# Where TensorE's queue issues the query-major scores in each attention step of an audio tower block

## The chip, the cores and the metric

The program runs on one core of a Trainium2 chip. The metric is the device time of one execution in microseconds (us), taken as the median of several runs; lower is better.

## The reference, cut to what matters

The input of 32 x 1024 samples is cut into patches of 16, which gives 2048 tokens (64 for each of 32 batch rows). Three stages follow, all in float32:

```python
h = silu(x_cat @ W_h.T + b_h) @ W_o.T + b_o + x_cat @ W_r.T + b_r      # (2048, 256)
# attention, 16 heads of 16, over the 64 tokens of one batch row
q, k, v = (einsum('bshd,ed->bshe', layernorm(h), W) for W in (Wq, Wk, Wv))
h = h + softmax(q k^T / sqrt(256)) v @ W_out.T + b_out
# a frequency-domain product; for real input it is one 256 x 256 matrix and a bias
h = h + real(ifft(fft(layernorm(h)) @ w_freq)) + bias
```

## The kernel before, in words

The 2048 tokens are 16 tiles of 128 tokens (two batch rows each); T is 16. A first stage (to about 44 us) makes h for all tiles. From then on one step per tile does the attention and the frequency product, software-pipelined: in `step(i)` each engine works at several tiles at once.

TensorE's queue is written out by hand: `step(i)` at line 1213 calls the parts in a fixed order, and each part first waits on semaphores for its inputs. An engine works its queue strictly in that order. The parts, with their lines:

- `turn_side(i-1)`, line 1096 (matmuls at 1101): two transposes of the residual tile h2, wanted by the frequency product.
- `turn_max(i+1)`, line 1089 (matmul at 1093): one transpose of the row maxima.
- `turn_x(i+3)`, line 1174 (matmuls at 1180): two transposes of the normalized tile. In step 1, tile 4 is turned ahead of the side. These are the three turns.
- `scores(i+2)`, line 1052 (matmuls at 1058), behind the two waits of `scores_inputs(i+2)`, line 1048: the query-major scores of tile i+2, 16 small matmuls of 32 rows by 64 columns of the array, which a profile shows as 32 records. They go to columns 0 to 255 of banks 0 to 3 and serve for nothing but the row maxima.
- `keyed_scores(i+1)` (1073) and `take_max(i+1)` (1085): the key-major scores of tile i+1 in columns 256 to 511 of the same banks, and the maxima taken off.
- `mix_freq(i-1)` (1133 with the leading part, 1137 with the rest), `project(i)` (1166 leading, 1170 rest), `query(i+3)` (1189 to 1191).
- `weigh(i+1)`, line 1105 (sums at 1113, weighing at 1120), the last of the step.

ScalarE (ACT), `step` at 404: `copy_max(i+1)` (374), `copy_side(i-1)` (388, 391), `copy_xT(i+3)` (358), `lead_on(i)` (395), `exponent(i+1)` (380, four), `copy_q(i+3)` (368), `copy_xzT(i+3)` (363, two). VectorE (DVE), `step` at 896: `divide(i)` (853 to 867), `variance2(i-1)` (890, 894), `split_x(i+3)` (789), four `maximum(i+2)` (835), `split_max(i+2)` (842, 844), `residual(i)` (886, makes h2), `finish(i-1)` (877, makes y). A `maximum` of tile i+2 waits for its scores and, besides, for the exponent of tile i+1 on the same bank (line 834). GpSimd (POOL), `step` at 604: `place_same(i+2)` (552), `split_side(i-1)` (591), `split_on(i)` (602), `inv_std2(i-1)` (566, 570), `add_bias(i-1)` (576), `normalize(i+4)` (584). SyncE (SP) issues two transfers of `place_crossed(i+2)` (297) and one store (289) in each step.

Of the kernel before, what the change touches and what calls it, by code (L numbers as in the profile page):

```python
# [24 lines left out]
T = BATCH * TOK // P  # L25
# [3 lines left out]
QUADS = 4  # L29
# [34 lines left out]
def audio_tower_kernel(nc, a, out):  # L64
    with ExitStack() as ctx:
# [3 lines left out]
        def sem(name):  # L69
            return ctx.enter_context(nc.semaphore(name))  # L70
# [145 lines left out]
        scores_done, max_done, max_turned, max_copied = (  # L216
            sem("scores_done"), sem("max_done"), sem("max_turned"), sem("max_copied"))
# [718 lines left out]
        def _(pe):  # L936
# [111 lines left out]
            def scores_inputs(t):  # L1048
                pe.wait_ge(xzT_copied, 2 * (t + 1))
                pe.wait_ge(q_copied, t + 1)  # L1050

            def scores(t):

                for half in range(HALF):
                    for b in range(2):
                        for j in range(QUADS):
                            rows32 = slice(32 * j, 32 * j + 32)
                            last = pe.matmul(bank[j][TOK * b:TOK * b + TOK, half * P:(half + 1) * P],  # L1058
                                             qT[t % 3][rows32, half, TOK * b:TOK * b + TOK],
                                             xzT[t % 3][rows32, 2 * half + b, :, :].rearrange("p e k -> p (e k)"),  # L1060
                                             start=True, stop=True)
                            if half == HALF - 1 and b == 1:
                                last.then_inc(scores_done, 1)

            def keyed_scores(t):

                for half in range(HALF):
                    for b in range(2):
                        for j in range(QUADS):
                            rows32 = slice(32 * j, 32 * j + 32)  # L1070
                            at0 = D + half * P + TOK * b
                            for e in range(2):
                                pe.matmul(bank[j][TOK * e:TOK * e + TOK, at0:at0 + TOK],  # L1073
                                          xzT[t % 3][rows32, 2 * half + b, e, :],
                                          qT[t % 3][rows32, half, TOK * b:TOK * b + TOK],
                                          start=(half == 0 and b == 0), stop=False, skip_group_check=True)

            def take_max(t):

                pe.wait_ge(max_copied, HALF * (t + 1))  # L1080
                if t == 0:
                    pe.wait_ge(minus_set, 1)
                for j in range(QUADS):
                    rows32 = slice(32 * j, 32 * j + 32)
                    pe.matmul(bank[j][:, D:2 * D], minus_rows[rows32, :],  # L1085
                              maxT[rows32, :, :].rearrange("p h q -> p (h q)"),
                              start=False, stop=True, skip_group_check=True).then_inc(keyed_done, 1)

            def turn_max(t):
                pe.wait_ge(max_lo_set, t + 1)  # L1090
                if t == 0:
                    pe.wait_ge(h_copied, T - 1)
                pe.transpose(bank[MAX_BANK][:, 0:P], max_terms[:].rearrange("p j r -> p (j r)").bitcast(F32),  # L1093
                             ident[:]).then_inc(max_turned, 1)

            def turn_side(t):
                pe.wait_ge(h2_done, t + 1)
                if t == T - 1:
                    pe.wait_ge(side_copied, t)
                for half in range(HALF):  # L1100
                    last = pe.transpose(bank[SIDE_BANK][:, D + half * P:D + (half + 1) * P],  # L1101
                                        h2[t % 2][:, half * P:(half + 1) * P], ident[:])
                last.then_inc(side_turned, 1)
# [21 lines left out]
            def mix_freq(t):  # L1125
                pe.wait_ge(side_copied, t + 1)
                if t == 0:
                    pe.wait_ge(mix_split, 1)
                if t >= 1:
                    pe.wait_ge(y_set, t)  # L1130
                for half in range(HALF):
                    for w in (mix_hi, mix_lo):
                        pe.matmul(bank[FREQ_BANK][:, D:2 * D], side_hi[:, half * P:(half + 1) * P], w[:, half, :],  # L1133
                                  start=(half == 0 and w is mix_hi), stop=False)
                pe.wait_ge(side_lo_set, t + 1)
                for half in range(HALF):
                    last = pe.matmul(bank[FREQ_BANK][:, D:2 * D], side_lo[:, half * P:(half + 1) * P], mix_hi[:, half, :],  # L1137
                                     start=False, stop=(half == HALF - 1))
                last.then_inc(freq_done, 1)
# [12 lines left out]
            def project(t):  # L1152
                if t == 0:
                    pe.wait_ge(mix_kept, 1)
                if t >= WHOLE_ON:
                    pe.wait_ge(on_set, t + 1)
                    for half in range(HALF):
                        last = pe.matmul(bank[LAST_PROJ_BANK if t == T - 1 else PROJ_BANK][:, 0:D], onT[:, half, :],  # L1158
                                         value_whole[:, half, :],
                                         start=(half == 0), stop=(half == HALF - 1))  # L1160
                    last.then_inc(proj_done, 1)
                    return
                pe.wait_ge(on_hi_set, t + 1)
                for half in range(HALF):
                    for w in (value_hi, value_lo):
                        pe.matmul(bank[PROJ_BANK][:, 0:D], on_hi[:, half, :], w[:, half, :],  # L1166
                                  start=(half == 0 and w is value_hi), stop=False)
                pe.wait_ge(on_lo_set, t + 1)
                for half in range(HALF):
                    last = pe.matmul(bank[PROJ_BANK][:, 0:D], on_lo[:, half, :], value_hi[:, half, :],  # L1170
                                     start=False, stop=(half == HALF - 1))
                last.then_inc(proj_done, 1)

            def turn_x(t):
                pe.wait_ge(xh_set, t + 1)
                if t >= 1:
                    pe.wait_ge(q_copied, t)
                    pe.wait_ge(xzT_copied, 2 * t)
                for half in range(HALF):
                    last = pe.transpose(bank[X_BANK][:, half * P:(half + 1) * P], xh[t % 2][:, half * P:(half + 1) * P],  # L1180
                                        ident[:])
                last.then_inc(x1_turned, 1)

            def query(t):
                pe.wait_ge(x_lo_set, t + 1)
                if t == 0:
                    pe.wait_ge(score_split, 1)
                out_q = bank[QUERY_BANK][:, D:2 * D]
                pe.matmul(out_q, score_hi[:], x_hi[:], start=True, stop=False)
                pe.matmul(out_q, score_lo[:], x_hi[:], start=False, stop=False)  # L1190
                pe.matmul(out_q, score_hi[:], x_lo[:], start=False, stop=True).then_inc(q_done, 1)  # L1191
# [19 lines left out]
                pe.matmul(half, halfway[:, 1, c * P:(c + 1) * P], sine[:], start=False, stop=True).then_inc(mixw_done, 1)  # L1211

            def step(i):
                if i == 1:
                    turn_x(4)
                if i >= 1:
                    turn_side(i - 1)
                if 0 <= i + 1 < T:
                    turn_max(i + 1)
                if 0 <= i < T - 3 and i != 1:  # L1220
                    turn_x(i + 3)
                if 0 <= i + 2 < T:
                    scores_inputs(i + 2)
                    scores(i + 2)
                if 0 <= i + 1 < T:
                    keyed_scores(i + 1)
                    take_max(i + 1)
                if 1 <= i < T - 2:
                    mix_freq(i - 1)
                if i >= 0:  # L1230
                    project(i)
                if 0 <= i + 3 < T:
                    query(i + 3)
                if i == -1:
                    cols_spectrum(1)
                if 0 <= i + 1 < T:
                    weigh(i + 1)
# [40 lines left out]
            for i in range(-1, T - 1):  # L1278
                step(i)
# [37 lines left out]
```

## Time and profile before

| | |
|---|---|
| median of 3 runs | 139.19 us (138.58 to 139.27) |
| the profiled execution, its own time | 140.0 us |
| its span in the trace | 138.2 us |
| TensorE busy | 130.9 us, 95% |
| VectorE / ScalarE / GpSimd busy | 111.2 / 91.4 / 94.2 us |
| granted TensorE clock | 1.0 throughout |

Times are us from the start of the span. A row of the timeline gives start, duration, engine, line and operation, what is written from what is read, the shape and the count; brackets at its end tell how long the engine had been idle before it and who ended that. PE is TensorE's matmuls, PEld its weight loads. The duration of one matmul includes its way through the array, so consecutive matmuls overlap, and what a matmul costs is read from start to start. The end of a matmul is modelled.

### The profile page before, as it was taken

How to read it: one execution, taken by the hardware profiler on the slowest of the kernel's cores; microseconds unless marked ns; L12 is line 12 of the kernel's file. 1: busy time of each engine (PE TensorE's matmuls, PEld its weight loads, DVE VectorE, ACT ScalarE, POOL GpSimd, SP SyncE). 2: the span in 40 equal slices, each digit the busy share in tenths (PEclk: the TensorE clock that was granted, in tenths of full speed). 3: DMA queues.
4: the chain of work that ended last, by engine and by line, in shares of the span. 5: the costliest groups of instructions: out<-in, count | busy, mean ns of one | idle time of the engine just before them, and what ended most of it. 6: DMA issues, size and time to landing. Idle time of an engine off the chain costs nothing.

```text
span 138.2 us, 7034 instructions
## 1 busy us (share of the span) xinstructions
PE 130.9 (95%) x2891; PEld 110.1 (80%) x2891; DVE 111.2 (80%) x337; ACT 91.4 (66%) x261; POOL 94.2 (68%) x186
## 2 busy tenths in 40 slices
PE   6899999999999999999999999999999999998980
PEld 2389999999997876988888888788888888886640
DVE  4685499869979579897898898988988988988850
ACT  5376475478878676886867867768778678666110
POOL 3285895999547364678678787786796787774660
PEclk9999999999999999999999999999999999999999
DMA  3667000030000020221312302203112123031012
GB/s 62 164 159 261 20 0 0 5 34 9 2 0 5 5 24 0 24 48 21 62 38 24 61 15 50 55 12 66 44 18 57 47 24 61 1 66 43 0 47 72
DMA packets 24512, 5.89 MB, mean 43 GB/s; under 512 B 20384, under 2 KB 24224, under 8 KB 24480
## 3 DMA queue, kind: packets, MB, share of 16 engines
q1 hardware_dynamic: 24192, 5.31, 17.9%
q8 instruction: 23, 0.38, 1.2%
q10 hardware_dynamic: 288, 0.13, 0.4%
q14 instruction: 9, 0.07, 0.2%
HBM read 2.29 MB, written 2.10 MB: 32 GB/s over the span
## 4 chain that ended last, share of the span: by engine, by line
PE 77%; POOL 8%; issue 4%; DVE 4%; ACT 3%; ACTq 1%; POOLq 0%; DVEq 0%
PE bank L978 10%; PE bank L1073 7%; PE bank L1058 6%; PE bank L1113 5%; PE bank L983 5%; PE bank L1133 5%; PE bank L1120 4%; PE bank L1166 4%; PE bank L1101 3%; PE bank L972 3%; PE bank L1085 3%; PE bank L1170 2%; PE bank L1180 2%; PE bank L1137 2%; PE bank L1158 2%
## 5 line engine op out<-in xcount | busy, mean ns | idle before, releaser
L835 DVE TENSOR_REDUCE bank<-bank 128x4 f32<-128x256 f32 x64 | 22.8, 425 | 7.2 <-ACT pT L380 7.0
L380 ACT ACTIVATE pT<-bank 128x256 f32<-128x256 f32 x64 | 19.4, 390 | 3.8 <-PE bank L1085 3.6
L591 POOL TENSOR_TENSOR side_lo<-sideT,side_hi 128x256 fp32r<-128x256 f32 x14 | 10.3, 732 | 13.4 <-ACT sideT L391 13.4
L1073 PE MATMUL bank<-qT,xzT 32*64 32x64 f32 x1024 | 16.3, 234 | 0.0
L552 POOL TENSOR_SCALAR xblk<-xh,parity_sb 128x128 f32<-128x128 f32 x32 | 11.5, 375 | 6.9 <-PE bank L1120 5.6
L705 DVE TENSOR_TENSOR hid_lo<-bank,hid_hi 128x512 fp32r<-128x512 f32 x16 | 10.9, 684 | 6.3 <-ACT bank L342 6.3
L1073 PEld LDWEIGHTS bank<-qT,xzT 32*64 32x64 f32 x1024 | 15.5, 130 | 0.3 <-issue 0.2
L374 ACT ACTIVATE maxT<-bank,parity_sb 128x128 fp32r<-128x128 f32 x32 | 10.0, 363 | 8.6 <-PE bank L1093 8.6
L560 POOL TENSOR_TENSOR hb_all<-h_all,bout_bc 128x256 f32<-128x256 f32 x16 | 11.6, 740 | 3.9 <-ACT h_all L346 3.9
L341 ACT ACTIVATE hid_hi<-bank 128x512 fp32r<-128x512 f32 x16 | 9.6, 599 | 5.3 <-PE bank L972 5.3
L368 ACT ACTIVATE qT<-bank 128x256 f32<-128x256 f32 x16 | 6.2, 386 | 9.6 <-PE bank L1191 9.6
L978 PE MATMUL bank<-wo_hi,hid_hi 128*128 128x256 f32 x64 | 11.7, 303 | 0.2
L576 POOL TENSOR_TENSOR h2b<-h,fbias_bc 128x256 f32<-128x256 f32 x16 | 11.7, 734 | 0.3 <-DVE h L886 0.3
L1120 PEld LDWEIGHTS bank<-pT,xblk 128*32 128x32 f32 x512 | 9.5, 110 | 2.7
L363 ACT ACTIVATE xzT<-bank,parity_sb 128x256 f32<-128x256 f32 x28 | 11.7, 472 | 0.0
L1058 PE MATMUL bank<-xzT,qT 32*64 32x128 f32 x512 | 11.1, 280 | 0.2 <-DVE hid_lo L705 0.2
L570 POOL TENSOR_TENSOR rstd<-ve,half_neg 128x1 f32<-128x1 f32 x16 | 9.1, 570 | 2.2
L602 POOL TENSOR_TENSOR on_lo<-onT,on_hi 128x256 fp32r<-128x256 f32 x14 | 10.4, 741 | 0.1
L1113 PE MATMUL bank<-pT,pair_ones_sb 128*32 128x256 f32 x128 | 10.2, 391 | 0.0
L983 PE MATMUL bank<-wo_hi,hid_lo 128*128 128x256 f32 x64 | 10.2, 281 | 0.0
L978 PE MATMUL bank<-wo_lo,hid_hi 128*128 128x256 f32 x64 | 10.1, 282 | 0.0
L1120 PE MATMUL bank<-pT,xblk 128*32 128x64 f32 x512 | 10.1, 219 | 0.0
(170 smaller groups left out, 379.4 us busy)
## 6 DMA issues: line engine op xcount, KB each, us to landing
out<-y SPq DMA_DIRECT2D x16, 128.0 KB, 1.7
xblk<-xh SPq DMA_DIRECT2D x32, 32.0 KB, 2.5
wo_raw<-in_W_o SPq DMA_DIRECT2D x1, 512.0 KB, 4.1
wout_raw<-in_W_out SPq DMA_DIRECT2D x1, 256.0 KB, 3.0
fr<-in_wr SPq DMA_DIRECT2D x1, 256.0 KB, 4.2
fi<-in_wi SPq DMA_DIRECT2D x1, 256.0 KB, 4.4
bout_bc<-in_b_out SPq DMA_DIRECT2D x1, 128.0 KB, 3.4
cosine_sb<-in_cosine SPq DMA_DIRECT2D x1, 128.0 KB, 4.2
```

The lines of the kernel that those rows point to most:

```text
L363: nc.scalar.activation(xzT[t % 3][:, :, e, :], bank[X_BANK][:, 0:D].rearrange("p (g k) -> p g k", k=TOK), ACT.Copy, scale=parity[:, e:e + ...
L380: nc.scalar.activation(pT[:, j, :], bank[j][:, D:2 * D], ACT.Exp).then_inc(exp_done, 1)
L552: last = nc.gpsimd.tensor_scalar(xblk[t % 2][:, b, :].rearrange("p (g e d) -> p g e d", e=2, d=HD)[:, :, b, :], xh[t % 2][:].rearrange("p ...
L560: nc.gpsimd.tensor_tensor(hb_all[:, t, :], h_all[:, t, :], bout_bc[:], ALU.add).then_inc(hb_done, 1)
L576: nc.gpsimd.tensor_tensor(h2b[t % 2][:], h2[t % 2][:], fbias_bc[:], ALU.add).then_inc(h2b_done, 1)
L835: nc.vector.tensor_reduce(rowmax[:, j, :], bank[j][:, 0:D].rearrange("p (h k) -> p h k", k=TOK), AX_X, ALU.max).then_inc(max_done, 1)
L978: pe.matmul(bank[MIX_BANK[par]][:, 0:D], hid_hi[:, par, c * P:(c + 1) * P], w[:, c, :], start=(t < 2 and c == 0 and w is wo_hi), stop=False)
L983: last = pe.matmul(bank[MIX_BANK[par]][:, 0:D], hid_lo[:, par, c * P:(c + 1) * P], wo_hi[:, c, :], start=False, stop=(t > 0 and c == NC - 1))
L1058: last = pe.matmul(bank[j][TOK * b:TOK * b + TOK, half * P:(half + 1) * P], qT[t % 3][rows32, half, TOK * b:TOK * b + TOK], xzT[t % 3][row ...
L1073: pe.matmul(bank[j][TOK * e:TOK * e + TOK, at0:at0 + TOK], xzT[t % 3][rows32, 2 * half + b, e, :], qT[t % 3][rows32, half, TOK * b:TOK * b ...
L1113: last = pe.matmul(sums[32 * j:32 * j + 32, D:2 * D], pair_ones[:], pT[:, j, :], start=True, stop=True)
L1120: last = pe.matmul(bank[PV_BANK][32 * j:32 * j + 32, cols], xblk[t % 2][:, b, half * P + 32 * j:half * P + 32 * j + 32], pT[:, j, cols], s ...
```

## The change

In steps 0 to 13 the scores of tile i+2 with their input waits are issued first, directly behind `weigh(i)` of the step before and ahead of the turns, and a wait for all maxima of tile i+1 (`max_done`) is put ahead of them. Before, `turn_max(i+1)`, which waits for the split maxima, stood ahead and implied it. Step -1 keeps its order. Nothing else is changed; no instruction is added but the wait.

```diff
             def step(i):
+                if 0 <= i and i + 2 < T:
+                    pe.wait_ge(max_done, QUADS * (i + 2))
+                    scores_inputs(i + 2)
+                    scores(i + 2)
                 if i == 1:
                     turn_x(4)
                 if i >= 1:
@@ -1219,7 +1223,7 @@
                     turn_max(i + 1)
                 if 0 <= i < T - 3 and i != 1:
                     turn_x(i + 3)
-                if 0 <= i + 2 < T:
+                if i == -1:
                     scores_inputs(i + 2)
                     scores(i + 2)
                 if 0 <= i + 1 < T:
```

## Rows read from the trace of the kernel before

**Rows 1.** The page: busy time and share of each engine.

```profile
PE 130.9 (95%) x2891; PEld 110.1 (80%) x2891; DVE 111.2 (80%) x337; ACT 91.4 (66%) x261; POOL 94.2 (68%) x186
```

**Rows 2.** The chain that ended last, over step 9 (start us, us, what).

```profile
97.83 0.45 PE bank L1120 x32
98.28 0.37 PE bank L1101 x2
...
98.97 0.62 PE bank L1058 x32
...
103.25 0.45 PE bank L1120 x32
```

**Rows 3.** Windows: steps 5 to 13 with their boundary, and the end.

```profile
core 0: us, PE busy (x) PEld busy (x) DVE busy (x) ACT busy (x) POOL busy (x), PEclk, DMA share, GB/s
...
70.86:119.89 49.03, 49.03 (x1447) 41.93 (x1441) 43.76 (x136) 36.66 (x118) 37.30 (x72) 1.00 0.21 40
...
124.95:138.20 13.25, 8.67 (x137) 5.77 (x137) 7.43 (x20) 3.13 (x10) 5.19 (x10) 1.00 0.13 41
```

**Rows 4.** Timeline where step 8 ends and step 9 begins.

```profile
97.30 0.38 ACT L368 ACTIVATE qT<-bank 128x256 f32<-128x256 f32 x1 [0.77 <-PE bank L1191]
...
97.58 0.83 ACT L363 ACTIVATE xzT<-bank,parity_sb 128x256 f32<-128x256 f32 x2
...
98.20 0.20 PEld L1101 LDWEIGHTS bank<-ident,h 128*128 128x128 f32 x2
```

**Rows 5.** Timeline of step 13's start.

```profile
119.61 0.48 ACT L363 ACTIVATE xzT<-bank,parity_sb 128x256 f32<-128x256 f32 x1
119.89 0.20 PEld L1101 LDWEIGHTS bank<-ident,h 128*128 128x128 f32 x2
```

**Rows 6.** Timeline of step 1's start, where a turn waits for an ACT copy.

```profile
53.76 0.48 ACT L363 ACTIVATE xzT<-bank,parity_sb 128x256 f32<-128x256 f32 x1
...
54.35 0.20 PEld L1180 LDWEIGHTS bank<-ident,xh 128*128 128x128 f32 x2 [0.41 <-issue]
```

**Rows 7.** Timeline of step 3's start, which waits for the residual.

```profile
64.95 0.48 ACT L363 ACTIVATE xzT<-bank,parity_sb 128x256 f32<-128x256 f32 x1
...
65.43 0.20 PEld L1101 LDWEIGHTS bank<-ident,h 128*128 128x128 f32 x2 [0.30 <-DVE h L886]
```

**Rows 8.** Timeline of step 9: turn, scores, key-major scores.

```profile
98.70 0.27 PE L1180 MATMUL bank<-ident,xh 128*128 128x128 f32 x1
...
98.90 0.69 PE L1058 MATMUL bank<-xzT,qT 32*64 32x128 f32 x32
...
99.39 1.01 PE L1073 MATMUL bank<-qT,xzT 32*64 32x64 f32 x64
```

**Rows 9.** Timeline of the first stage's end: scores followed by a full-array matmul.

```profile
41.69 0.70 PE L1058 MATMUL bank<-xzT,qT 32*64 32x128 f32 x32 [0.16 <-DVE hid_lo L705]
...
42.32 0.10 PEld L989 LDWEIGHTS bank<-wr_termsT,x_termsT 128*128 128x128 bf16 x1 [0.17 <-issue]
```

**Rows 10.** Timeline of step 8: the side's remainder and its reader.

```profile
94.63 0.73 POOL L591 TENSOR_TENSOR side_lo<-sideT,side_hi 128x256 fp32r<-128x256 f32 x1 [0.84 <-ACT sideT L391]
...
95.68 0.31 PEld L1137 LDWEIGHTS bank<-mix_hi,side_lo 128*128 128x128 f32 x2
```

**Rows 11.** Timeline of step 0: TensorE waits for a POOL remainder.

```profile
51.45 0.74 POOL L602 TENSOR_TENSOR on_lo<-onT,on_hi 128x256 fp32r<-128x256 f32 x1
...
52.24 0.30 PEld L1170 LDWEIGHTS bank<-value_hi,on_lo 128*128 128x128 f32 x2 [0.22 <-POOL on_lo L602]
```

**Rows 12.** The chain that ended last, steps 13 and 14.

```profile
124.15 0.74 POOL h2b L576
...
124.92 0.48 DVE y L877
...
127.04 1.13 PE bank L1158 x4
```

**Rows 13.** Waits: line waited for, total us, times, longest us.

```profile
DVE bank L835 <- ACT pT L380: 7.0, 15, 1.6
...
PEld bank L1101 <- DVE h L886: 1.0, 3, 0.4
```

## The prediction

> **What bounds the kernel now.** I first read the page: TensorE is busy for 95% of the span [rows 1]. Busy time alone proves little for overlapping matmuls, so I read the chain that ended last next. Over a steady step it never leaves TensorE: each group starts where the one before it ended, and from one weighing to the next it takes 103.25 - 97.83 = 5.42 us [rows 2]. The windows say the same: from the start of step 4 at 70.86 to that of step 13 at 119.89 are 9 steps in 49.03 us, and no moment without a matmul [rows 3]. So in steps 4 to 13 whatever is added between two matmuls is added to the time, and nothing is there to be won by filling waits. Only steps 0 to 3 and the end have short waits.
>
> **What moves.** In steps 0 to 13 the 16 scores matmuls (32 records) go ahead of turn_side, turn_max and turn_x in TensorE's queue. They issue no DMA, and no instruction on ACT, DVE, POOL or SP changes its place. The scores' own price, 0.49 us from start to start [rows 8], is paid before and after. Their consumers gain nothing from having them early: `maximum` also waits for the exponent of the tile before, and it is this that ends its wait 15 times [rows 13]; that exponent hangs on take_max, still behind the turns. The new wait on max_done costs nothing: the maxima are done before the residual starts, which in its turn is done before the turns start. Three things do cost.
>
> **Term 1, the inputs of the scores.** The scores of step i read xzT and q of tile i+2, which ACT copies at the end of step i-1: query ends, copy_q starts at 97.30, the two xzT copies run from 97.58 for 0.83 us, to 98.41 [rows 4]. TensorE meanwhile has only the weighing, and is ready for the next step at 98.20. Before, three turns covered the copy. From the end of such a copy to TensorE's first weight load that waited for it are 54.35 - (53.76 + 0.48) = 0.11 us [rows 6]. So the scores start at 98.52, a wait of 0.32. I took it for the steps 2 to 13, 12 of them; the last reads 119.61 + 0.48 + 0.11 - 119.89 = 0.31 [rows 5]. In step 3 the kernel already stands for the residual, to 65.43, and the copy would be usable at 64.95 + 0.48 + 0.11 = 65.54: only 0.11 is new there [rows 7]. Step 1 already waits for this same copy ahead of turn_x(4) [rows 6], and step 0 has its copies long before. The sum is 11 x 0.32 + 0.11 = 3.6 us. The stall doesn't repay itself: the next query is behind the scores, and the next copies behind that query. Queued behind the waiting scores are all three turns, and behind those ACT's copies of maxima, side and x.
>
> **Term 2, one more change of the array's shape.** Turns use the full array (128*128), scores and keyed scores tiles of 32*64, so scores to keyed is free now. A turn costs 0.11 and the scores start 0.20 behind the last turn's start, so full to small costs 0.09 [rows 8]; after the change turn to keyed scores pays that in its place. New is scores to turn. The trace has that direction once, where the first scores precede a full-array matmul: 42.32 - 41.69 = 0.63, against 0.49 in front of keyed scores [rows 8, 9], so 0.14. It could be as little as 0 if that row hid some other wait, or as much as 0.20 if everything must leave the array (98.90 + 0.69 - 99.39, the modelled end against the next start [rows 8]). I take 0.14, the one direct row. Times 14 steps, 2.0 us. The step from weighing to scores replaces weighing to turn and lies under the wait of term 1, in which the array empties anyway. The Trainium skill, "TensorEngine Tiling (Array Packing)", section "Tiling Modes", says that changing the tiling mode drains the TensorE. With a whole drain for each added change the term would be 14 x 0.20 = 2.8 us; the row speaks for less, since the weight load at 42.32 comes before the modelled end at 42.39 [rows 9].
>
> **Term 3, the side's remainder loses its cover.** turn_side starts a relay: ACT copies maxima, then side twice, POOL makes side_lo, and TensorE's second part of mix_freq reads it. Now POOL is done at 94.63 + 0.73 = 95.36 and TensorE loads it at 95.68 [rows 10]: 0.32 of slack, less the 0.05 that TensorE needed after a POOL remainder in step 0 (52.24 - 51.45 - 0.74 [rows 11]). With the scores no longer between turn_side and mix_freq TensorE arrives 0.49 earlier in the relay's time: 0.49 - 0.32 + 0.05 = 0.22 us of wait, in steps 1 to 13. The bounds are 0 (if the relay also shrinks) and 0.33 (if the wake-up takes 0.11 more before the matmul itself can start, then late by that much). on_lo, behind side_lo on POOL, is late by no more than that, so the wait at mix_freq covers it. The maxima keep cover: two copies of ACT against turn_x and about 0.9 us of keyed scores.
>
> **The end.** Behind step 13 the chain leaves TensorE: it runs over POOL's h2b, DVE's y and divide, to project(14) at 127.04 [rows 12]. This relay counts from turn_side(13), which now comes 0.32 + 0.49 + 0.14 = 0.95 later after the weighing. So step 13 counts 0.95 instead of 0.68. Nothing in steps 14 and 15 gives the 0.49 back.
>
> **The sum.** Step 0: 0.14. Step 1: 0.14 + 0.22 = 0.36. Steps 2 to 12: 11 x (0.32 + 0.14 + 0.22) = 7.48, less 0.21 in step 3. Step 13: 0.95. Together 8.7 us. The profiled execution took 140.0 (span 138.2, 1.8 around it) and would take 148.7. The median of the runs is 0.8 below that execution, so I forecast 139.2 + 8.7 = 147.9 us. A steady step would be 6.1 us instead of 5.42.
>
> **The rivals.**
> 1. *The relay of the side keeps up*, terms 1 and 2 only. For it: 0.22 is a difference of small numbers, and the order of ACT might shift in TensorE's favour. 14 x 0.14 + 3.6 + 0.49 = 6.1, so 145.3. Chance 0.15.
> 2. *Only the shape change costs*, if ACT's copies are in time after all. Against: they end after the weighing in every step from 2 on [rows 4, 5]. 139.2 + 2.0 = 141.2. Chance 0.05.
> 3. *POOL and DVE close a longer loop.* h2b, y, divide and onT all hang on turn_side, and if they also come late for the next on_hi, each step pays more than 6.1. For it: that relay bounds the end now [rows 12]. Against: ACT reaches on_hi only behind five copies that themselves wait for the turns, so onT may come later together with them. At an assumed 0.15 more in each of 12 steps, 149.7. Chance 0.07.
> 4. *The clock falls.* With two waits per step TensorE might be granted 1.2 instead of 2.4 GHz, and a half-clock step would cost up to 5 us more: beyond 153. Against: over the last 13.25 us it is busy for only 8.67 and is granted 1.00 throughout [rows 3]. Chance 0.02.
> 5. *Faster.* turn_side waits for DVE's residual three times, 1.0 us in all by the weight loads [rows 13]; the scores would cover that. It decides if the xzT copies end before the weighing and the added shape change is free. Then about 0.5 of it is true gain (the rest is pipelining of the loads): 138.7. Against: rows 4 has the copy 0.21 too late before any wake-up. Chance 0.03.
> 6. *Gain and cost cancel*, a small cost of shapes against that same gain, 139.2. Chance 0.01.
>
> **How the numbers follow.** The forecast has 0.67. About 0.5% either way is what a measurement of this kernel can tell from no change, 0.7 us. Faster has rival 5, 0.03; same takes rival 6 and the part of rival 2 in which the shape change costs next to nothing, 0.02; slower is the rest, 0.95. The range takes in rival 1 with a shape change at half price (145.3 - 1.0 = 144.3) and, above, the whole drain (+0.8) and the longer wake-up of term 3 (13 x 0.11 = 1.4): 150.1. Outside stand most of rival 2 and rivals 4 to 6, some 0.1, and the cases in which I mis-sized the terms by more than their bounds, which I put at another 0.1.
>
> **What would show it.** Each step right: weight loads of L1058 wait for ACT xzT about 0.3 in 12 steps; 0.63 from scores to the first turn; L1137 waits for POOL side_lo about 0.2; a steady period of 6.1; clock 1.00. Wrong: a period under 5.6 with L1058 directly behind the weighing, which would mean that the copies aren't late; or L1137 without a wait, which is rival 1; or waits at L1166 or L1170 for onT's copies, which is rival 3.

## The result, and the profile after

| | before | after |
|---|---|---|
| median | 139.23 us (4 runs, 138.58 to 140.02) | 147.63 us (4 runs, 147.06 to 148.18) |
| ratio | | 1.058, 95% interval 1.054 to 1.063 |
| profiled execution, own time / span | 140.0 / 138.2 us | 147.31 / 144.8 us |
| first to last weighing group (L1120), 15 steps | 80.00 us | 88.11 us |

The forecast was 147.9 us with a range of 144.3 to 150.1. On the median the change costs 8.4 us, and 8.1 by the ratio. The spans differ by only 6.6 us, because two things outside the steps differ between these two executions: the first stage ended 0.43 us earlier in the one of after, and from the end of the last y to the end of the span it took 2.2 us against 3.3. The steps themselves are the 8.11 us to explain. The ratios here leave out an execution that took over 1.5% longer than the fastest of its kernel; there is one, 142.19 us, and it is the profiled one of `shape_in_changed`.

First the page of after, its busy line; it answers to [rows 1].

```profile
PE 134.7 (93%) x2891; PEld 109.1 (75%) x2891; DVE 112.6 (78%) x337; ACT 89.8 (62%) x261; POOL 94.3 (65%) x186
```

The same instructions, and TensorE is now busy for 93% where it was busy for 95%: that says nearly nothing. The chain that ended last does, over one steady step; it answers to [rows 2].

```profile
101.96 0.45 PE bank L1120 x32
102.41 0.23 issue
102.64 0.70 PE bank L1058 x32
103.34 0.37 PE bank L1101 x2
103.71 0.11 PE bank L1093
103.82 0.22 PE bank L1180 x2
104.03 0.84 PE bank L1073 x53
104.88 0.32 PE bank L1085 x4
105.20 0.67 PE bank L1133 x4
105.87 0.03 issue
105.90 0.50 PE bank L1137 x2
```

Two "issue" entries are new, 0.23 behind the weighing and 0.03 in front of L1137. "Issue" is time for which the profile shows nobody to wait for. What ended each has to be read from the timeline of after around them: ACT's copy, and POOL's remainder.

```profile
101.71 0.83 ACT L363 ACTIVATE xzT<-bank,parity_sb 128x256 f32<-128x256 f32 x2
101.78 0.63 PE L1120 MATMUL bank<-pT,xblk 128*32 128x64 f32 x32
...
102.61 0.48 PEld L1058 LDWEIGHTS bank<-xzT,qT 32*64 32x64 f32 x32 [0.37 <-issue]
...
103.27 0.44 PE L1101 MATMUL bank<-ident,h 128*128 128x128 f32 x2
...
103.97 0.91 PE L1073 MATMUL bank<-qT,xzT 32*64 32x64 f32 x64
...
104.81 0.39 PE L1085 MATMUL bank<-maxT,minus_rows_sb 32*128 32x256 f32 x4
...
105.11 0.74 POOL L591 TENSOR_TENSOR side_lo<-sideT,side_hi 128x256 fp32r<-128x256 f32 x1 [1.53 <-ACT sideT L391]
```

The copies end at 101.71 + 0.83 = 102.54, and the first load of the scores comes at 102.61. From the weighing group to the scores are 0.86 us (101.78 to 102.64). In the kernel before it is 0.56 from the weighing to the turns, in the timeline of [rows 4]:

```profile
97.65 0.63 PE L1120 MATMUL bank<-pT,xblk 128*32 128x64 f32 x32
...
98.21 0.44 PE L1101 MATMUL bank<-ident,h 128*128 128x128 f32 x2
```

POOL's remainder ends at 105.11 + 0.74 = 105.85, and L1137 starts at 105.90. The other new wait is named in the list of waits of after (total us, times, longest us).

```profile
PEld bank L1058 <- issue: 5.0, 14, 0.4
...
PEld bank L1137 <- POOL side_lo L591: 3.2, 13, 0.3
```

It comes 13 times, mostly with 0.24, once in each of the steps 1 to 13, which are those with a turn of the side and this second part of `mix_freq`. The windows of after give 9 steady steps, from the scores of step 4 to those of step 13.

```profile
core 0: us, PE busy (x) PEld busy (x) DVE busy (x) ACT busy (x) POOL busy (x), PEclk, DMA share, GB/s
...
72.29:126.89 54.60, 52.17 (x1440) 41.58 (x1440) 45.35 (x136) 35.70 (x117) 37.38 (x72) 1.00 0.19 36
```

54.60 / 9 = 6.07 us a step at a granted clock of 1.00, against 49.03 / 9 = 5.45 in [rows 3]. (The 5.45 contains one pause of TensorE; without it the step is 5.42.)

### The profile page after: what moved, and what is told of

Read it like the earlier page. It is cut to its first block, busy times and chain, and to the rows that moved or that the text cites. A ratio compares the mean times of both kernels' runs of the same rounds, so it can differ in the third digit from the quotient of the medians.

```text
span 144.8 us, 7034 instructions
## 1 busy us (share of the span) xinstructions
PE 134.7 (93%) x2891; PEld 109.1 (75%) x2891; DVE 112.6 (78%) x337; ACT 89.8 (62%) x261; POOL 94.3 (65%) x186
## 4 chain that ended last, share of the span: by engine, by line
PE 78%; issue 6%; POOL 4%; DVE 3%; ACT 3%; DMA 3%; ACTq 1%; SPq 0%; POOLq 0%; DVEq 0%
PE bank L978 10%; PE bank L1073 7%; PE bank L1058 6%; PE bank L1113 6%; PE bank L1133 5%; PE bank L983 5%; PE bank L1137 4%; PE bank L1120 4%; PE bank L1166 4%; PE bank L1101 3%; PE bank L972 3%; PE bank L1085 3%; DMA xblk<-xh 3%; PE bank L1180 2%; PE bank L1170 2%
## 5 line engine op out<-in xcount | busy, mean ns | idle before, releaser
L1073 PE MATMUL bank<-qT,xzT 32*64 32x64 f32 x1024 | 14.7, 231 | 0.0
L1073 PEld LDWEIGHTS bank<-qT,xzT 32*64 32x64 f32 x1024 | 12.6, 130 | 2.5 <-issue 2.5
L1058 PEld LDWEIGHTS bank<-xzT,qT 32*64 32x64 f32 x512 | 7.7, 131 | 5.5 <-issue 5.0
L1120 PEld LDWEIGHTS bank<-pT,xblk 128*32 128x32 f32 x512 | 9.5, 110 | 2.8
L789 DVE TENSOR_TENSOR x_lo<-bank,x_hi 128x256 fp32r<-128x256 f32 x16 | 6.8, 424 | 6.1 <-ACT x_hi L358 5.9
L584 POOL TENSOR_SCALAR xh<-h_all,rstd,shift 128x256 f32<-128x256 f32 x16 | 8.9, 554 | 2.4 <-DMA xblk<-xh 1.7
```

Of the source, the lines that this page charges most:

```text
L1073: pe.matmul(bank[j][TOK * e:TOK * e + TOK, at0:at0 + TOK], xzT[t % 3][rows32, 2 * half + b, e, :], qT[t % 3][rows32, half, TOK * b:TOK * b ...
L1120: last = pe.matmul(bank[PV_BANK][32 * j:32 * j + 32, cols], xblk[t % 2][:, b, half * P + 32 * j:half * P + 32 * j + 32], pT[:, j, cols], s ...
```

## The experiments

Steps are measured from one L1120 group to the next (in kernels with two more lines ahead of it, L1122). A steady step is one of steps 4 to 12 without a pause of TensorE; the pauses are in the last section. "Sum" is the 15 steps from the first such group to the last, in the profiled execution. Ratios are to the kernel before on the same chip.

### The waits alone: waits_only

```diff
             def step(i):
+                if 0 <= i and i + 2 < T:
+                    pe.wait_ge(max_done, QUADS * (i + 2))
+                    scores_inputs(i + 2)
                 if i == 1:
                     turn_x(4)
```

> The order of the kernel before, with only the waits (maxima, xzT and q of tile i+2) put at the head of steps 0 to 13; the scores stay behind the turns. Theory of three additive terms: only term 1 is left, 11 x 0.30 + 0.1 in step 3 and 0.3 at the end, so about 139.2 + 3.6 = 142.8 us, a steady period of 5.73, and no wait at L1137. Rival, a closed loop over ACT and POOL sets the period of 6.06 as soon as TensorE is late for the turns: near 147, with a wait at L1137. Rival, the late start is won back because the turns and scores are short: under 140.

Measured: 141.81 us, ratio 1.016 (1.012 to 1.020); sum 83.14, steady step mostly 5.68 to 5.70. In this kernel the profile names the releaser, at the matmul of the turn behind the waits; its timeline at a step's start:

```profile
99.58 0.63 PE L1120 MATMUL bank<-pT,xblk 128*32 128x64 f32 x32
100.44 0.41 PE L1101 MATMUL bank<-ident,h 128*128 128x128 f32 x2 [0.23 <-ACT xzT L363]
```

The wait for xzT is real by itself and adds 0.27 to the step: 0.30 in front of the turn, less 0.03 that the turns then take less. L1137 doesn't wait: from L1133 to it are 0.58 us, as in the kernel before. So there is no closed loop that would take the step to 6.06. The ratio gives 2.2 us (1.6 to 2.8), the trace 3.1; what may lie between them is in the last section.

### The input wait taken away: no_input_wait

```diff
                     pe.wait_ge(max_done, QUADS * (i + 2))
-                    scores_inputs(i + 2)
-                    scores(i + 2)
+                    scores_inputs(i + 1)
+                    scores(i + 1)
```

> The changed order, but the scores at the head of step i read tile i+1 (its copies are a whole step old), so the maxima belong to the wrong tile; the same matmuls are issued. Three additive terms: term 1 goes, L1120 to L1058 is 0.56 instead of 0.86, so 12 x 0.30 = 3.6 less than the changed kernel, about 144.0 us, period 5.76, L1137 still waits 0.24. Rival, a closed loop over ACT and POOL: the wait reappears further down the step and the time stays near 147.5.

Measured: 143.51 us, ratio 1.028 (1.023 to 1.032); sum 84.39, steady step 5.75. The scores stand directly behind the weighing now, 0.56 behind the start of its group:

```profile
99.80 0.63 PE L1120 MATMUL bank<-pT,xblk 128*32 128x64 f32 x32
100.36 0.69 PE L1058 MATMUL bank<-xzT,qT 32*64 32x128 f32 x32
```

Term 1 is 0.31 a step, and it goes without coming back elsewhere. The wait for `max_done` is still in this kernel, so it costs nothing. Step 7 alone has 6.14, by a pause in its keyed scores.

### The remainder waits taken away: no_remainder_waits and no_side_wait

```diff
-                pe.wait_ge(side_lo_set, t + 1)
                 for half in range(HALF):
-                    last = pe.matmul(bank[FREQ_BANK][:, D:2 * D], side_lo[:, half * P:(half + 1) * P], mix_hi[:, half, :],
+                    last = pe.matmul(bank[FREQ_BANK][:, D:2 * D], side_hi[:, half * P:(half + 1) * P], mix_hi[:, half, :],
...
-                pe.wait_ge(on_lo_set, t + 1)
                 for half in range(HALF):
-                    last = pe.matmul(bank[PROJ_BANK][:, 0:D], on_lo[:, half, :], value_hi[:, half, :],
+                    last = pe.matmul(bank[PROJ_BANK][:, 0:D], on_hi[:, half, :], value_hi[:, half, :],
```

`no_remainder_waits` has both hunks, and a wait on ACT for the side_lo of the tile before, ahead of the side_hi copy, which is long fulfilled. `no_side_wait` has the first hunk alone.

> The changed order, but mix_freq and project read side_hi and on_hi again in place of the remainders side_lo and on_lo, without waiting for them (POOL still computes them); the products lose their low-order part. Three additive terms: term 3 goes, which the trace of the changed kernel shows as 0.19 + 0.12 = 0.31 a step, 13 times: 4.0 less, about 143.6 us, period 5.75; the scores' wait for xzT stays at about 0.3. Rival, closed loop: the wait grows at another place and the time stays above 146.5.

Measured: 143.77 us, ratio 1.030 (1.026 to 1.035); sum 84.16, steady step 5.75. Term 3 is 0.31 a step too. The sum has two things besides. Step 0 is 0.29 shorter (4.64 against 4.93), because its wait for on_lo, which the kernel before has too [rows 11], is left out as well. And at the end nothing is won: step 13 is 0.35 shorter and step 14 is 0.35 longer.

> The changed order; only mix_freq reads side_hi again in place of side_lo, without its wait; project still waits for on_lo, which POOL makes right behind side_lo. I expect nearly nothing: on_lo lands 0.70 behind side_lo, and TensorE reaches L1170 0.70 behind L1137, so the wait moves from L1137 to L1170: 147.4 us, with about 0.3 at L1170. Rival, only the wait for side_lo counts, as my term 3 had it: 4.0 less, 143.6 us.

Measured: 148.25 us, ratio 1.061 (1.056 to 1.067); sum 87.97, steady step 6.06, as in the changed kernel. Its list of waits has in place of L1137's the following row (L1169 is this kernel's second part of `project`):

```profile
PEld bank L1169 <- POOL on_lo L602: 3.2, 14, 0.3
```

The wait is the same size one group later. POOL finishes on_lo 0.70 us behind side_lo and TensorE reaches the one group 0.70 behind the other, so the two waits are one lateness, and the profile shows only the one met first. Who had read L1137 off the list and mended that alone would have gained nothing.

### Only the order left: shape_in_changed

The edits of `no_input_wait` and `no_remainder_waits` together.

> The changed order without the input wait (scores read tile i+1) and without both remainder waits (side_hi and on_hi read again), so only the order itself is left. If the terms are additive: 147.6 - 3.6 - 4.0 = 140.0 us, period about 5.46, of which the shape change is 14 x 0.04 and the rest the end's relay. If the shape change costs 0.14 net: 141.2. If something else in the order costs: more than 141.5.

Measured: 139.88 us, ratio 1.000 (0.997 to 1.003), 10 runs; sum 80.62, steady step 5.44 to 5.45. In the trace the new order alone costs 0.03 in a steady step. The other steps are not alike. Step 0 is 0.27 shorter than before, since the on_lo wait of the kernel before is left out here too. Step 3 is 0.18 shorter (5.45 against 5.63), since the scores now cover the wait for the residual. Steps 13 and 14 are 0.21 and 0.41 longer. Without the pauses of both traces (some 0.4 us here, 0.25 before) it adds up to 0.4 us, at the edge of what the runs resolve; with the gain of step 0, which isn't the order's, set aside it would be 0.7. The steps of this profiled execution begin later, the first L1120 at 49.98 against 48.1 to 48.8 in the other profiles, so that its span is no measure of them. The timeline of one step's start shows the parts:

```profile
98.97 0.63 PE L1122 MATMUL bank<-pT,xblk 128*32 128x64 f32 x32
99.53 0.69 PE L1060 MATMUL bank<-xzT,qT 32*64 32x128 f32 x32
100.15 0.44 PE L1103 MATMUL bank<-ident,h 128*128 128x128 f32 x2
```

### Two changes of shape more: shape_only

```diff
                     turn_max(i + 1)
-                if 0 <= i < T - 3 and i != 1:
-                    turn_x(i + 3)
                 if 0 <= i + 2 < T:
                     scores_inputs(i + 2)
                     scores(i + 2)
+                if 0 <= i < T - 3 and i != 1:
+                    turn_x(i + 3)
```

> The order of the kernel before, with the scores moved ahead of turn_x alone: turn_side, turn_max, scores, turn_x, keyed scores. Their inputs are ready there (0.39 behind the weighing's end against 0.32), and the scores still stand between turn_side and mix_freq, so only the added change of the array's shape is left, in 12 steps. By the 0.14 of my term 2: 139.2 + 1.7 = 140.9 us. By what the trace of the changed kernel shows (scores 0.14 longer, keyed scores 0.10 shorter, net 0.04): 139.7 us, period 5.46. By a whole drain of 0.20: 141.6.

Measured: 140.90 us, ratio 1.009 (1.006 to 1.012), 8 runs; sum 81.97, steady step 5.59 to 5.60. The timeline of a steady step of this kernel:

```profile
99.69 0.27 PE L1093 MATMUL bank<-ident,max_terms 128*128 128x128 f32 x1
99.89 0.69 PE L1058 MATMUL bank<-xzT,qT 32*64 32x128 f32 x32
100.52 0.44 PE L1180 MATMUL bank<-ident,xh 128*128 128x128 f32 x2
100.88 0.84 PE L1073 MATMUL bank<-qT,xzT 32*64 32x64 f32 x58
```

The expectation was badly set up. By parting the three turns this kernel has two changes of shape more than the kernel before: turns, scores, turn, keyed scores. The changed kernel has only one more. Read as two it fits: 0.63 - 0.49 = 0.14 from scores to turn; 0.36 for two transposes and the way into the keyed scores, where two transposes alone take 0.22, so 0.14; and keyed scores that take 0.84 and not 0.94, 0.10 less. That is 0.18 a step, and 5.60 - 5.42 is 0.18. By the ratio it is 1.2 us (0.8 to 1.6) over 12 steps, by the trace 2.0. That the median, 140.9, is the very number expected from 0.14 a step is a coincidence: two changes stand behind it, not one.

### Repairs that leave nothing out: query_early, side_first, both_repairs

```diff
+                if 0 <= i and i + 3 < T:
+                    query(i + 3)
                 if i >= 0:
                     project(i)
-                if 0 <= i + 3 < T:
+                if i == -1:
                     query(i + 3)
```

> The changed order, and query(i+3) ahead of project(i) in steps 0 to 12, so that ACT copies q and xzT 0.7 us earlier; nothing is left out. Three additive terms: xzT is there before the weighing ends, term 1 goes by a change that computes everything: 3.6 less, about 144.0 us, and L1137 still waits. Rival, ACT is still in the exponents: then copy_q starts at their end, and part of the wait stays, 145.5. Rival, closed loop: 147.

Measured: 143.64 us, ratio 1.029 (1.023 to 1.035); sum 83.96, steady step 5.76. The copies now end at 98.61 + 0.83 = 99.44 in the step where the weighing group starts at 99.38, well before the scores at 99.94:

```profile
98.61 0.83 ACT L363 ACTIVATE xzT<-bank,parity_sb 128x256 f32<-128x256 f32 x2
...
99.38 0.63 PE L1120 MATMUL bank<-pT,xblk 128*32 128x64 f32 x32
...
99.94 0.23 PEld L1058 LDWEIGHTS bank<-xzT,qT 32*64 32x64 f32 x16
```

Term 1 is gone by another way than in `no_input_wait` and is worth the same in a steady step. Step 0 gains 0.26 besides (4.67 against 4.93), since `query` there stands in front of the group that waits for on_lo and covers the wait.

```diff
                 if i + 1 < T:
-                    copy_max(i + 1)
+                    act.wait_ge(max_turned, i + 2)
                 if i >= 1:
                     copy_side(i - 1)
+                if i + 1 < T:
+                    copy_max(i + 1)
```

> The changed order; on ACT the two side copies go ahead of the two maxima copies, once the turn of the maxima is done (nothing is left out). The side reaches POOL two copies (0.5 us) earlier, so the wait at L1137 (0.31 a step with its loads) goes; the maxima come 0.5 later, for which the trace of the changed kernel has about 0.4 of cover in front of L1085, so up to 0.2 may come back there. By additive terms: period 5.75 to 5.95, 2 to 4 us less than the changed kernel, 143.5 to 145.5 us. Rival, a closed loop over ACT and POOL: 147.5.

Measured: 147.74 us, ratio 1.059 (1.052 to 1.065); sum 88.13, steady step 6.02 to 6.05: a miss. The wait for the side is gone, and one for the maxima has come, in its list of waits (L1087 is this kernel's `take_max`):

```profile
PEld bank L1087 <- ACT maxT L374: 5.4, 14, 0.6
...
PE bank L1087 <- ACT maxT L374: 3.5, 14, 0.4
```

The keyed scores take 1.11 us to take_max instead of 0.84. I had given the maxima 0.4 of cover; it was 104.81 - (103.85 + 0.63) = 0.33, less the wake-up, and they were moved back by two copies, 0.5. As I read it, ACT's copies behind the turns take about as long as the work that TensorE has left in front of their readers, so whichever reader is served last waits: 0.31 a step for the side, 0.27 for the maxima.

> The changed order with query ahead of project and the side copies ahead of the maxima copies; nothing is left out. Additive terms: 147.6 - 4.0 (term 1, as measured) - 2 to 4 (as side_first), so 139.8 to 141.6 us, period 5.46 to 5.65. It can't beat the kernel before, whose period is TensorE's own 5.42. Rival: with both repairs some wait that was hidden comes out, and the time is above 142.5.

Measured: 144.01 us, ratio 1.032 (1.025 to 1.039); steady step 5.73, hardly less than the 5.76 of `query_early` alone. The expectation counted a gain that `side_first` doesn't have.

### The end: last_step_old

```diff
-                if 0 <= i and i + 2 < T:
+                if 0 <= i and i + 3 < T:
                     pe.wait_ge(max_done, QUADS * (i + 2))
...
-                if i == -1:
+                if i in (-1, T - 3):
                     scores_inputs(i + 2)
```

> The changed order in steps 0 to 12, the old order in step 13. In the changed kernel step 13 took 0.88 more than before and step 14 0.07 more; both should go: 147.6 - 0.9 = 146.7 us. Rival, the end's relay over POOL and DVE absorbs what step 13 adds: no change, 147.6.

Measured: 146.20 us, ratio 1.047 (1.041 to 1.053); sum 87.18, with 4.84 for step 13 and 4.40 for step 14, which before are 4.83 and 4.39. The new order in step 13 costs 0.93 in the trace; the medians differ by 1.4 us and the ratios by 1.1%, 1.5 us, with intervals of half a per cent each way.

### Both kernels once more: before_again, after_again

> The kernel before, profiled once more, to see how much of its trace repeats: from the first to the last L1120 group 80.0 us again, a period of 5.42, and whether the 3.3 us between the last y and the end of the span (2.2 in the changed kernel's trace) belong to the kernel or to this one execution.

Measured: 140.76 us, span 139.0; the sum is 81.10, not 80.00. The period is 5.40 to 5.43 in all the steps 4 to 12 but two. From the end of the last y to the end of the span it takes 2.2 us, as in all other profiles, so the 3.3 of the first profile belonged to that one execution and not to the kernel.

> The changed kernel, profiled once more, for the same purpose: 88.1 us from the first to the last L1120 group, a period of 6.06, and 2.2 us from the last y to the end.

Measured: 147.91 us, span 145.2, sum 88.10 again, and 2.2 us from the last y to the end. What makes before's sum differ is in the last section.

## Why the prediction was right

The sum of the steady step closes from separate runs. Before 5.42; the order alone +0.03 (`shape_in_changed`); the inputs of the scores +0.31 (6.06 - 5.75, `no_input_wait`; `query_early` says 0.30); the remainders +0.31 (6.06 - 5.75, `no_remainder_waits`): 6.07, measured 6.06. So in the steady steps the terms add up; each wait lies at another place of TensorE's queue. At the end they don't: there `no_remainder_waits` only moved 0.35 from step 13 to step 14. Point by point:

- **What bounds the kernel** held: with the waits of terms 1 and 3 taken out of the changed order the steady step is 5.45 against 5.42 and the ratio 1.000. The ratio flatters a little, since the wait of step 0, 0.27, is left out with them.
- **Nothing is won by early scores** held. In the changed order the maxima wait for the exponent all the same, and a steady step has no part that became shorter but the keyed scores.
- **Term 1** was right: 0.32 forecast, 0.31 by the run. Of its parts the wake-up, from the copy's end to TensorE's load, was 0.07 and not 0.11, and the matmul then stands 0.03 behind its load. That three turns covered the copies before isn't right: `turn_x(i+3)` waits for the same copies of tile i+2 itself, and in step 9 of the kernel before its first load stands at 98.52, 0.11 behind their end at 98.41. Two turns covered them and little was to spare, which doesn't change the term. In step 3 the wait of before for the residual was covered as forecast: 5.63 became 6.06, 0.43 more, where the other steady steps have 0.64.
- **Term 2** was mis-sized: 0.14 a step forecast, 0.03 measured. The 0.14 from scores to turn is there to the digit (103.27 - 102.64 = 0.63). The step that failed is the sentence that scores to keyed scores "is free now". It wasn't: the keyed scores take 0.94 behind the scores and 0.84 behind a turn, so that 0.10 of the new price comes back. Why they take less behind a turn no run shows. The Trainium skill, "TensorEngine Tiling (Array Packing)", section "Tiling Modes", has a drain at each change of mode. The traces agree that a change between the turns and the small tiles costs something in either direction, 0.09 to 0.14, and `shape_only`, which has two more of them, pays 0.14 for each. In the changed order 0.10 of the added price is given back, which no count of mode changes shows.
- **Term 3** was mis-sized the other way: 0.22 forecast, 0.31 measured. The place and the cause were right. The wait is 0.19 in front of L1137 (0.77 from L1133 where before are 0.58). The rest, 0.11, comes behind it: load and matmul of L1137 start together at 105.90, so the matmul hasn't its load done in advance, and L1137 to L1166 is 0.34, not 0.23. That is the upper bound that the prediction named and didn't take. The timeline of [rows 11] already had it, in the row behind the load at 52.24, where two matmuls of this form that wait for a remainder take 0.51 and not 0.40:

```profile
52.24 0.51 PE L1170 MATMUL bank<-value_hi,on_lo 128*128 128x256 f32 x2
```

  That the wait of mix_freq covers on_lo held, and `no_side_wait` shows how exactly.
- **Step 0** cost nothing, not 0.14: 4.93 in both traces. **Step 1** cost 0.57, not 0.36: the leading part of mix_freq waits there for the side copies too (0.49 from L1085 to L1133 where 0.32 is usual).
- **The end** cost 0.88 in step 13 and 0.07 in step 14, together the 0.95 forecast, and `last_step_old` gives 0.93 back. In `shape_in_changed`, where the 0.32 of term 1 isn't paid, the two steps cost 0.21 + 0.41 = 0.62, which is the 0.49 + 0.14 of the forecast. The turn that this relay starts from is the one that step 13 issues, `turn_side(12)`: its side_lo begins at 121.72 in the chain that ended last. The prediction calls it `turn_side(13)`, which is a slip of the index and changes no number.

By the steps: 0 + 0.57 + 0.60 + 0.43 + 9 steps of 6.06 to 6.08 against 5.42 (one of them 5.68) = 5.58, + 0.88 + 0.07 = 8.1 us, where 8.7 was forecast. Term 2 was 1.5 too high over 14 steps and term 3 was 1.2 too low over 13. That they nearly cancel is luck, and the forecast's closeness (0.3 us) is not the measure of how well its terms were known.

Of the rivals: the relay of the side did not keep up (rival 1); the copies were not in time (rivals 2, 5 and 6), and of rival 5's gain only the 0.2 of step 3 was left; no longer loop closed (rival 3), since there is no wait at L1166 in the steady steps, and a wait taken away came back only at on_lo in `no_side_wait`, in full, and in `side_first`, whose new order on ACT makes the maxima late, with 0.27 of 0.31. The clock stayed at 1.00 over the steady steps (rival 4).

## What to carry to other kernels

In a queue that is full, a group that stands between a turn and the reader of its copy is cover; before moving it, read for each result that others wait for how late it lands against where it would then be read, in front of the group and behind it. When two remainders come from one engine one after the other, the profile names only the first as waited for: take both away before believing a repair. And a group's price from start to start holds only beside the neighbours that it has in that trace: the keyed scores were 0.10 us cheaper with a turn in front of them than with the scores.

## What the runs showed of the hardware that I had not expected

**Pauses inside one group.** In the kernel before the 64 keyed-score records of step 7 take 1.21 us in the first profile and 1.90 in the second, where 0.93 is usual. The timeline of the second:

```profile
88.27 0.95 PE L1073 MATMUL bank<-qT,xzT 32*64 32x64 f32 x60
89.91 0.33 PE L1073 MATMUL bank<-qT,xzT 32*64 32x64 f32 x4 [0.69 <-issue]
```

Nothing that the profile shows was waited for. A second pause, 0.45 us, came in step 11 of that execution. The 0.69 more in step 7 and the 0.45 in step 11 are the whole difference between the sums of 80.00 and 81.10. `shape_only` and `no_input_wait` pause in the same step 7 (1.11 and 1.54 where 0.84 is usual). In the second profile of the changed kernel the keyed scores of that step take 1.05 instead of 0.84, and yet the step has 6.06: the wait for side_lo in front of L1137 shrinks by the same 0.2 (L1133 to L1137 is 0.58, not 0.78). A kernel that waits for others hides such a pause, and one that TensorE bounds pays it in full. That may be why the ratios put `waits_only` and `shape_only` 0.8 to 0.9 us nearer to the kernel before than the traces do, if unprofiled executions of before pause more than its first profile. No run separates that, and what the pauses are stays open.

**The last stores.** In the second profile of before the last y waits 1.45 us for a store to land, and so it does in four other profiles: `shape_only` 1.50, `last_step_old` 1.67, `side_first` 1.83, `shape_in_changed` 1.90. In the others it waits 0.69 for TensorE. The two profiles of before differ in it and the two of after don't. In the first profile of before, in turn, the time behind the last y was 1.1 us longer than in any other. From the last L1120 group to the end of the span it takes 8.6 to 9.8 us over all the profiles, which is a reason to compare the steps and not the spans.
